# Streamed units shifted between the positions of a lap, and narrow convolution tiles cut to the pieces they need

## The chip, the cores and the metric

The kernel runs on one core of one Trainium2 chip. The metric is device time in microseconds (us) of one execution; lower is better. Engines: TensorE (PE; its weight loads are listed as PEld), VectorE (DVE), ScalarE (ACT), GpSimd (POOL), and SyncE (SP), which issues most loads.

## The reference

Two layers over x of shape 1 x 16 x 2048 x 2048 (f32):

```python
# layer 0: _gn is a group norm over pairs of channels; one 6 x 11 depthwise filter per channel
xm = where(tril(ones(H, W)), _gn(x), 0)
y  = conv(xm, weight, padding=((5, 0), (5, 5)), feature_group_count=C)
x  = x + where(tril(ones(H, W)), y, 0)
# layer 1: bias[c, i, j] = table[i - j + n - 1, c], table from a small network of the position
x  = x + (_gn(x) + bias)
```

So only the lower triangle of each channel is convolved and changed by layer 0, while both norms need sums over everything, and layer 1 touches every element.

## The kernel before

**Work.** A group is two channels (`CPG`), so there are 8 groups. A channel is cut into 4 bands of 512 rows; row = 4p + k, with p the partition and k = 0..3. The lower triangle of a band is walked in tiles of 128 columns that step by 118 (`STEP`): 5, 9, 13 and 18 tiles in bands 0 to 3, 45 per channel, 90 per group. Tile number n within the group, 0 to 89, is called its position (45 to 89 are the second channel). A tile is four pieces of 32 columns (`NPC`, `XC`). The last tile of a band is narrower: at positions 4, 44, 49 and 89 only two pieces hold columns of the band, at 13 and 58 three; the kernel before works on all four. A tile is "diagonal" (`is_diag`, 42 of 90) if it crosses the diagonal.

**A tile's way.** ACT normalizes it into `xn` (`norm`, L647, four tiles ahead); if diagonal, POOL multiplies `xn` by the mask (`mask_tile`, L1084); PE transposes four pieces into `psT` (L1170); ACT copies that as f16 into `XT` (`split_hi`, L659); DVE writes the f16 remainder (`split_lo`, L801); POOL moves two columns per piece through `halo` (L1099, L1110); PE does 36 matmuls into `psY`, nine per piece (L1184); DVE masks a diagonal tile in `psY` (L814) and adds it to x (`evict`, L816). `xn`, `psT`, `XT` and `psY` have three buffers each (`NB3`).

**Stages.** The program is a sequence of stages s, and each walks n = 0..89 on every engine. Stage s convolves group s - 1, collects the statistics of group s (bn_stats on DVE, L829) and finishes group s - 2 (norm 2 and bias). The time from the first eviction of a group to that of the next is called a lap here; laps 0 to 7 belong to groups 0 to 7.

**Streams.** What isn't held in SBUF passes through `ring`, 8 buffers of 512 KB. "a" units (58 per group, 0.5 MB loaded) are read for statistics by DVE: two bn_stats each. "u" units (36 per group, 0.5 MB loaded and 0.5 MB stored) are finished: 23 of them by ACT (scale, L708) and POOL (add bias, L1119), 13 by DVE alone (L1002). Kept blocks of bands 2 and 3 are finished in place by DVE (L991), stored by ACT's queue (L694), and then reloaded by SP for the next group (L572); `norm` of their first tile waits for the reload (tile 14, which ACT reaches at n = 10, and tile 18, at n = 14).

**The planner.** `plan` gives each u and a unit a position. `spread` fills, per position, the room that is left below a level after the other traffic; for u units the level is multiplied by `U_WEIGHT(n)`, and the a units are then spread with weight 1 over what the u units left. From these positions a loop over `wanted` fixes the ring buffer, the position of each load, use and store. A load of SP waits until the unit that held its buffer was stored or read, and SP's queue is in order: what stands behind it waits too. Stages 2 to 7 use this plan; in stages 8 and 9 the weight isn't used.

**PE's code.** Tiles go in triples, since buffers are taken modulo 3. Most triples run in hardware loops (`Fori`), the others are written out.

Of the kernel before, what the change touches and what calls it, by code (L numbers as in the profile page):

```python
# [25 lines left out]
def preact_conv_kernel(nc, x, wflip, w1, b1, w2, b2, w3, b3, out):  # L26
# [27 lines left out]
    def band_tiles(b):  # L54
# [73 lines left out]

    U_WEIGHT = lambda n: 1.8 if n < 10 else 1.5 if n > 82 else 1.0

# [177 lines left out]
    with ctx:  # L308
# [299 lines left out]
        def _(act):  # L608
# [45 lines left out]
            def split_hi(g, n):  # L654
                N = NT * g + n
                act.wait_ge(transposed, N + 1)
                wait(act, convolved, N - NB3 + 1)
                wait(act, halo_out, N - NB3 + 1)
                nc.scalar.copy(XT[:, n % NB3, 0, :, 2:P + 2], psT[n % NB3][:, :, :]).then_inc(hi_ready, 1)  # L659

# [119 lines left out]
        def _(dve):  # L780
# [282 lines left out]
        def _(pool):  # L1063
# [14 lines left out]
            def mask_tile(g, n):  # L1078
                c, b, t = TILES[n]
                pool.wait_ge(diag_normed, ND * g + DIAG_BEFORE[n] + 1)  # L1080
                v = xn[:, n % NB3, :, :, :]
                m = mask_at(b, t, 0, TIN)
                m = bass.AP(m.tensor, m.offset, [m.ap[0], [-XC, NPC], [1, K], [-1, XC]])
                nc.gpsimd.tensor_tensor(v, v, m, ALU.mult).then_inc(xn_ready, 1)  # L1084
# [16 lines left out]
            def halo_to(g, n):  # L1101

                c, b, t = TILES[n]
                N = NT * g + n
# [5 lines left out]
                nc.gpsimd.tensor_copy(halo[:, t, :, :, :], XT[:, n % NB3, :, :, P:P + 2]).then_inc(halo_out, 1)  # L1110

# [36 lines left out]
        def _(pe):  # L1148
# [15 lines left out]

            def transpose(N, m):

                wait(pe, lo_ready, N - NB3 + 1)
                pe.wait_ge(xn_ready, N + 1)
                for i in range(NPC):
# [19 lines left out]

            def triple(N, c, ahead=NB3, results_of=None):  # L1190

                for i in range(NB3):
                    if i < ahead:
                        transpose(N + i + 2, (i + 2) % NB3)
                    if i == 0 and results_of is not None:
                        sum_results(results_of)
                    convolve(N + i, i, c)

# [13 lines left out]
            def group(g, before, after):  # L1212

                first = NT * g
                pe.wait_ge(w_built, chan(g, 0) + 1)
                triple(first, 0, results_of=g - 1 if before else None)
                with pe.Fori(1, NTC // NB3) as j:
                    triple(first + NB3 * j, 0)
                pe.wait_ge(w_built, chan(g, 1) + 1)
                triple(first + NTC, 1)  # L1220
                with pe.Fori(NTC // NB3 + 1, SUM1[0] if after else 2 * NTC // NB3 - 1) as j:
                    triple(first + NB3 * j, 1)
                if after:
                    triple(first + NB3 * SUM1[0], 1)
                    sum_means(g + 1)
                    triple(first + NB3 * SUM1[1], 1)
                    sum_variances(g + 1)
                    with pe.Fori(SUM1[1] + 1, 2 * NTC // NB3 - 1) as j:
                        triple(first + NB3 * j, 1)

# [5 lines left out]
            for g in range(1, G - 1):  # L1236
                triple(NT * g - NB3, 1)
                group(g, True, True)
            triple(NT * (G - 1) - NB3, 1)
            group(G - 1, True, False)  # L1240
            triple(NT * G - NB3, 1, 1)
            sum_results(G - 1)
# [24 lines left out]
```

## Time and profile before

| what | value |
|---|---|
| median of 3 runs | 2638.41 us (2633.2 to 2640.93) |
| the profiled execution | 2638.45 us; its span 2636.7 us |
| DVE busy | 2304.3 us, 87% |
| PE busy | 1979.8 us, 75% |
| ACT / POOL busy | 1660.3 us, 63% / 1260.7 us, 48% |
| moved by DMA | 894.88 MB, mean 339 GB/s |

Busy time is the union of an engine's instructions; waiting, branching and issuing DMAs don't count. Group lines give count, busy time, mean duration, and the idle time before them with what ended it. In rows by stretch, DMA share is the mean busy share of the 16 DMA engines (it can come out slightly above 1), PEclk the granted TensorE clock.

### The profile page before, as it was taken

How to read it: one execution, taken by the hardware profiler on the slowest of the kernel's cores; microseconds unless marked ns; L12 is line 12 of the kernel's file. 1: busy time of each engine (PE TensorE's matmuls, PEld its weight loads, DVE VectorE, ACT ScalarE, POOL GpSimd, SP SyncE). 2: the span in 40 equal slices, each digit the busy share in tenths (PEclk: the TensorE clock that was granted, in tenths of full speed). 3: DMA queues.
4: the chain of work that ended last, by engine and by line, in shares of the span. 5: the costliest groups of instructions: out<-in, count | busy, mean ns of one | idle time of the engine just before them, and what ended most of it. 6: DMA issues, size and time to landing. Idle time of an engine off the chain costs nothing. (4 is left out here: it accounts for less than half of the span.)

```text
span 2636.7 us, 76763 instructions
## 1 busy us (share of the span) xinstructions
PE 1979.8 (75%) x28880; PEld 1876.5 (71%) x28880; DVE 2304.3 (87%) x4175; ACT 1660.3 (63%) x3051; POOL 1260.7 (48%) x1988
## 2 busy tenths in 40 slices
PE   4289988888687876878778877888868778899800
PEld 0289887878687776877778776787768778899800
DVE  7799988899888997899888998889988899778846
ACT  2167766766576675766667666666656757687722
POOL 1123235535545454454555445554554546475543
PEclk9999998999899999999898999999889998999955
DMA  9775649999899998999989998999989997797999
GB/s 337 273 243 170 233 136 384 393 371 351 329 408 377 380 337 332 402 359 385 354 334 396 359 366 329 378 392 362 348 329 395 384 373 297 284 355 274 334 370 360
DMA packets 313546, 894.88 MB, mean 339 GB/s; under 512 B 42272, under 2 KB 42272, under 8 KB 311296
## 3 DMA queue, kind: packets, MB, share of 16 engines
q1 hardware_dynamic: 198528, 576.64, 59.3%
q10 hardware_dynamic: 114832, 316.22, 31.0%
q8 instruction: 60, 0.98, 0.1%
q14 instruction: 126, 1.03, 0.1%
HBM read 576.36 MB, written 316.53 MB: 339 GB/s over the span
## 5 line engine op out<-in xcount | busy, mean ns | idle before, releaser
L1184 PEld LDWEIGHTS psY<-wsplit,XT 128*128 128x128 f16 x25920 | 1607.2, 102 | 355.9 <-DVE XT L801 128.6
L1184 PE MATMUL psY<-wsplit,XT 128*128 128x168 f16 (+5 forms) x25920 | 1635.9, 223 | 290.7 <-DVE XT L801 240.2
L659 ACT CAST XT<-psT 128x512 f16<-128x512 f32 x720 | 414.8, 576 | 561.0 <-PE psT L1170 325.5
L1110 POOL COPY halo<-XT 128x16 f16<-128x16 f16 x720 | 318.9, 443 | 657.5 <-DVE XT L801 647.3
L801 DVE TENSOR_TENSOR XT<-psT,XT 128x512 f16<-128x512 f32 x720 | 493.8, 686 | 140.3 <-ACT XT L659 139.4
L1084 POOL TENSOR_TENSOR xn<-xn,mask 128x512 f32<-128x512 f32 x336 | 423.7, 1261 | 387.5 <-ACT xn L647 325.8
L829 DVE BATCH_NORM_STATS2 entries<-ring 128x6 f32<-128x512 f32 x872 | 551.4, 679 | 61.3 <-DMA ring<-in_x 61.0
L1170 PE MATMUL psT<-ident,xn 128*128 128x128 f32 x2880 | 480.3, 292 | 98.2 <-POOL xn L1084 77.6
L1119 POOL TENSOR_TENSOR ring<-ring,bias 128x1024 f32<-128x1024 f32 x181 | 408.4, 2258 | 253.7 <-ACT ring L708 253.6
L647 ACT ACTIVATE xn<-kept_c_band,normp 128x512 f32<-128x512 f32 (+2 forms) x496 | 398.4, 803 | 48.3 <-DMA kept_c_band<-in_x 26.9
L1170 PEld LDWEIGHTS psT<-ident,xn 128*128 128x128 f32 x2880 | 317.8, 146 | 107.4 <-POOL xn L1084 72.5
L816 DVE SCALAR_TENSOR_TENSOR kept_c_band<-psY,wback,kept_c_band 128x472 f32<-128x472 f32 (+3 forms) x496 | 342.5, 691 | 14.2 <-PE psY L1184 7.3
L679 ACT ACTIVATE junk<-kept_c_band,cur 128x512 f32<-128x512 f32 (+2 forms) x464 | 311.6, 672 | 49.5 <-DVE kept_c_band L816 26.2
L991 DVE SCALAR_TENSOR_TENSOR kept_c_band<-kept_c_band,outp,bias 128x1024 f32<-128x1024 f32 x224 | 329.2, 1478 | 11.6 <-ACT bias L699 11.6
L708 ACT ACTIVATE ring<-ring,outp 128x1024 f32<-128x1024 f32 x181 | 206.0, 1140 | 124.1 <-DMA ring<-in_x 48.0
L814 DVE TENSOR_TENSOR psY<-psY,mask 128x472 f32<-128x472 f32 (+2 forms) x336 | 202.8, 604 | 11.7 <-PE psY L1184 11.4
L1002 DVE SCALAR_TENSOR_TENSOR ring<-ring,outp,bias 128x1024 f32<-128x1024 f32 x101 | 173.9, 1724 | 33.2 <-DMA ring<-in_x 24.3
L1099 POOL COPY XT<-halo 128x16 f16<-128x16 f16 x720 | 159.9, 222 | 51.4 <-PE psY L1184 47.4
L647 ACT ACTIVATE xn<-band,normp 128x512 f32<-128x512 f32 (+1 forms) x224 | 174.3, 779 | 13.9 <-DVE normp L911 13.9
L816 DVE SCALAR_TENSOR_TENSOR band<-psY,wback,band 128x472 f32<-128x472 f32 (+2 forms) x224 | 150.4, 671 | 6.3 <-PE psY L1184 0.7
L679 ACT ACTIVATE junk<-band,cur 128x512 f32<-128x512 f32 x192 | 131.9, 687 | 36.3 <-DVE band L816 27.1
L679 ACT ACTIVATION_READ_ACCUMULATOR junk<-kept_c_band,cur 128x1 f32 x464 | 87.1, 188 | 0.0
(81 smaller groups left out, 486.2 us busy)
## 6 DMA issues: line engine op xcount, KB each, us to landing
ring<-in_x SPq DMA_DIRECT2D x628, 512.0 KB, 8.6
out<-ring ACTq DMA_DIRECT2D x282, 512.0 KB, 6.1
kept_c_band<-in_x SPq DMA_DIRECT2D x224, 512.0 KB, 8.1
out<-kept_c_band ACTq DMA_DIRECT2D x224, 512.0 KB, 7.0
band<-in_x SPq DMA_DIRECT2D x48, 1024.0 KB, 11.3
out<-band ACTq DMA_DIRECT2D x45, 1024.0 KB, 8.7
ring<-out SPq DMA_DIRECT2D x90, 512.0 KB, 9.5
bias<-bias_scratch SPq DMA_DIRECT2D x16, 1793.5 KB, 8.5
```

The costliest lines, as they stand in the source:

```text
L647: last = nc.scalar.activation(to[:, :, 0:whole, :], slot(c, b)[:, :, x0:x0 + XC * whole].rearrange("p k (i c) -> p k i c", c=XC), ACT.Iden ...
L659: nc.scalar.copy(XT[:, n % NB3, 0, :, 2:P + 2], psT[n % NB3][:, :, :]).then_inc(hi_ready, 1)
L679: nc.scalar.activation(junk[:, 0:nr * (c1 - c0)].rearrange("p (r c) -> p r c", r=nr), slot(c, b)[:, r:r + nr, BW * q + c0:BW * q + c1], AC ...
L801: nc.vector.tensor_tensor(XT[:, n % NB3, 1, :, 2:P + 2], psT[n % NB3][:, :, :], XT[:, n % NB3, 0, :, 2:P + 2], ALU.subtract).then_inc(lo_r ...
L816: nc.vector.scalar_tensor_tensor(out=xs, in0=y, scalar=col(wback, c), in1=xs, op0=ALU.mult, op1=ALU.add, accum_out=sums[:, n:n + 1]).then_ ...
L829: last = nc.vector.bn_stats(entries[:, e, :], row(q, r))
L991: nc.vector.scalar_tensor_tensor(out=v, in0=v, scalar=col(outp, 0), in1=bias_at(blk, nr // 2 * h, nr // 2), op0=ALU.mult, op1=ALU.add).the ...
L1084: nc.gpsimd.tensor_tensor(v, v, m, ALU.mult).then_inc(xn_ready, 1)
L1110: nc.gpsimd.tensor_copy(halo[:, t, :, :, :], XT[:, n % NB3, :, :, P:P + 2]).then_inc(halo_out, 1)
L1119: nc.gpsimd.tensor_tensor(v, v, bias_at(STREAM[u]), ALU.add).then_inc(u_added, 1)
L1170: last = nc.tensor.transpose(psT[m][:, i, :], xn[:, m, i, :, :].rearrange("p k c -> p (k c)"), ident[:, :])
L1184: last = nc.tensor.matmul(psY[m][:, 0:rows, o + lo_c:o + hi_c], XT[:, m, xp, i, 2 - sh:2 - sh + P], wsplit[:, c, wp, K * sh:K * sh + rows, ...
```

## The change

Two things. The planner's weight of u units becomes 2.2 at positions 0 to 9 (was 1.8), 1.8 at 47 to 54 (was 1.0) and 1.2 from 83 on (was 1.5). And `split_hi`, `split_lo`, `halo_to`, the transposes and the convolution take `n_pieces[n]` pieces instead of four; `mask_tile` takes only the pieces from the diagonal's on, `evict` masks only the columns from the diagonal on. Since a loop of PE can't hold triples of different shape, `triples` loops only over runs of full ones (triples 5 to 13, 20 to 24, 27 and 28) and writes the others out.

```diff
+    n_pieces = [-(-min(TIN, BW * (b + 1) - STEP * t) // XC) for c, b, t in TILES]
+    left_of_diag = [max(0, BW * b - STEP * t) for c, b, t in TILES]
...
-    U_WEIGHT = lambda n: 1.8 if n < 10 else 1.5 if n > 82 else 1.0
+    U_WEIGHT = lambda n: 2.2 if n < 10 else 1.8 if 46 < n < 55 else 1.2 if n > 82 else 1.0
...
-                nc.vector.tensor_tensor(XT[:, n % NB3, 1, :, 2:P + 2], psT[n % NB3][:, :, :],
-                                        XT[:, n % NB3, 0, :, 2:P + 2], ALU.subtract).then_inc(lo_ready, 1)
+                np = n_pieces[n]
+                nc.vector.tensor_tensor(XT[:, n % NB3, 1, 0:np, 2:P + 2], psT[n % NB3][:, 0:np, :],
+                                        XT[:, n % NB3, 0, 0:np, 2:P + 2], ALU.subtract).then_inc(lo_ready, 1)
...
-                    nc.vector.tensor_tensor(y, y, mask_at(b, t, c0, c1), ALU.mult).then_inc(conv_masked, 1)
+                    d0 = max(c0, left_of_diag[n])
+                    y_diag = psY[n % NB3][:, :, d0:c1]
+                    nc.vector.tensor_tensor(y_diag, y_diag, mask_at(b, t, d0, c1), ALU.mult).then_inc(conv_masked, 1)
...
-                v = xn[:, n % NB3, :, :, :]
+                i0, i1 = left_of_diag[n] // XC, n_pieces[n]
+                v = xn[:, n % NB3, i0:i1, :, :]
...
-            def convolve(N, m, c):
+            def convolve(N, m, c, np=NPC):
...
-                products = [(i, sh, xp, wp) for i in range(NPC) for sh in range(3)
+                products = [(i, sh, xp, wp) for i in range(np) for sh in range(3)
...
+            def looped(j):
+                return all(n_pieces[(NB3 * j + i) % NT] == NPC for i in range(NB3 + 2))
```

By the new weights the units of stages 2 to 7 move. Per five positions, counts of uses before and after (a: statistics on DVE; D: u units finished by DVE; P: u units finished by ACT and POOL):

| positions | a | D | P |
|---|---|---|---|
| 0-4 | 5, 4 | 0, 0 | 2, 3 |
| 5-9 | 1, 1 | 1, 1 | 2, 3 |
| 10-14 | 1, 1 | 0, 0 | 1, 0 |
| 15-19 | 3, 3 | 0, 1 | 1, 0 |
| 20-24 | 5, 5 | 1, 0 | 0, 1 |
| 25-39 | 9, 9 | 2, 2 | 6, 6 |
| 40-44 | 6, 7 | 1, 1 | 1, 0 |
| 45-49 | 7, 5 | 0, 1 | 1, 2 |
| 50-54 | 2, 0 | 1, 0 | 0, 2 |
| 55-59 | 2, 1 | 0, 0 | 0, 0 |
| 60-64 | 3, 3 | 0, 0 | 0, 0 |
| 65-69 | 3, 4 | 0, 1 | 1, 0 |
| 70-74 | 2, 2 | 1, 0 | 2, 2 |
| 75-79 | 3, 4 | 1, 2 | 3, 2 |
| 80-84 | 3, 4 | 2, 2 | 3, 2 |
| 85-89 | 3, 5 | 3, 2 | 0, 0 |

The order on SP at the start of stage 4 (names: `ring` loads are a and u units, `kept_c0_band2` the reloads, `wstage` filter taps). Before:

```order
L566 DMA ring<-in_x 128x1024
L566 DMA ring<-in_x 128x2x512
L566 DMA ring<-in_x 128x1024
L572 DMA kept_c0_band2<-in_x 128x2x512 x2
L572 DMA kept_c0_band2<-in_x 128x1024
L592 DMA wstage<-taps_scratch 32x6x42 x4
L566 DMA ring<-in_x 128x1024
L572 DMA kept_c0_band2<-in_x 128x1024 x3
L566 DMA ring<-in_x 128x1024 x5
L572 DMA kept_c0_band3<-in_x 128x1024
```

And now:

```order
L570 DMA ring<-in_x 128x2x512 x2
L570 DMA ring<-in_x 128x1024 x4
L576 DMA kept_c0_band2<-in_x 128x2x512 x2
L576 DMA kept_c0_band2<-in_x 128x1024
L596 DMA wstage<-taps_scratch 32x6x42 x4
L576 DMA kept_c0_band2<-in_x 128x1024 x3
L570 DMA ring<-in_x 128x1024 x5
L570 DMA ring<-out_0 128x1024
L576 DMA kept_c0_band3<-in_x 128x1024
```

The ring load that stood between the taps and the second set of reloads is gone; the sixth and seventh u units (uses at n = 8 and 9, before at 13 and 18) now load ahead of the first reload. The last of them takes the buffer of this stage's first u unit, whose store is issued at n = 5.

On DVE, the same stage at tiles 48 to 50 (`psY0`, `psY1`, `psY2`), where L829 are the statistics and L991 the kept blocks. Before:

```order
L829 BN_STATS entries<-ring 128x6 x4
L814 TENSOR_TENSOR psY0<-psY0,mask 128x4x118
L816 SCALAR_TENSOR_TENSOR band0,sums<-psY0,wback,band0 128x4x118
L801 TENSOR_TENSOR XT<-psT0,XT 128x4x128
L991 SCALAR_TENSOR_TENSOR kept_c1_band2<-kept_c1_band2,outp,bias 128x1024
L829 BN_STATS entries<-ring 128x6 x4
L814 TENSOR_TENSOR psY1<-psY1,mask 128x4x35
L816 SCALAR_TENSOR_TENSOR band0,sums<-psY1,wback,band0 128x4x35
L801 TENSOR_TENSOR XT<-psT1,XT 128x4x128
L991 SCALAR_TENSOR_TENSOR kept_c1_band2<-kept_c1_band2,outp,bias 128x1024
L829 BN_STATS entries<-ring 128x6 x2
L816 SCALAR_TENSOR_TENSOR band1,sums<-psY2,wback,band1 128x4x123
```

And now:

```order
L837 BN_STATS entries<-ring 128x6 x2
L822 TENSOR_TENSOR psY0<-psY0,mask 128x4x118
L824 SCALAR_TENSOR_TENSOR band0,sums<-psY0,wback,band0 128x4x118
L807 TENSOR_TENSOR XT<-psT0,XT 128x4x128
L999 SCALAR_TENSOR_TENSOR kept_c1_band2<-kept_c1_band2,outp,bias 128x1024
L837 BN_STATS entries<-ring 128x6 x2
L822 TENSOR_TENSOR psY1<-psY1,mask 128x4x35
L824 SCALAR_TENSOR_TENSOR band0,sums<-psY1,wback,band0 128x4x35
L807 TENSOR_TENSOR XT<-psT1,XT 128x4x128
L999 SCALAR_TENSOR_TENSOR kept_c1_band2<-kept_c1_band2,outp,bias 128x1024
L824 SCALAR_TENSOR_TENSOR band1,sums<-psY2,wback,band1 128x4x123
```

Three pairs of statistics are gone from this short piece. On PE, tile 4 of the first group (`psY1`) is written out instead of being in the loop. Before, 36 matmuls in four pieces:

```order
L1184 MATMUL psY1<-wsplit,XT 128x4x37 x6
L1184 MATMUL psY1<-wsplit,XT 128x37 x3
L1184 MATMUL psY1<-wsplit,XT 128x4x42 x6
L1184 MATMUL psY1<-wsplit,XT 128x42 x3
L1184 MATMUL psY1<-wsplit,XT 128x4x42 x6
L1184 MATMUL psY1<-wsplit,XT 128x42 x3
L1184 MATMUL psY1<-wsplit,XT 128x4x32 x6
L1184 MATMUL psY1<-wsplit,XT 128x32 x3
```

And now, with the transposes around it, 18 in two:

```order
L1180 MATMUL psT0<-ident,xn 128x128 x4
L1194 MATMUL psY1<-wsplit,XT 128x4x37 x6
L1194 MATMUL psY1<-wsplit,XT 128x37 x3
L1194 MATMUL psY1<-wsplit,XT 128x4x42 x6
L1194 MATMUL psY1<-wsplit,XT 128x42 x3
L1180 MATMUL psT1<-ident,xn 128x128 x4
```

The third and fourth pieces are gone.

## Rows read from the trace of the kernel before

**Rows 1.** Laps 0, 3, 7: us, busy PE PEld DVE ACT POOL, PEclk, DMA share, GB/s.

```profile
125.20:384.20 259.00, 234.98 (x3682) 230.15 (x3679) 238.08 (x501) 179.31 (x359) 77.36 (x226) 0.97 0.58 195
1008.80:1321.60 312.80, 246.07 (x3606) 234.40 (x3606) 284.05 (x521) 205.43 (x380) 160.18 (x247) 0.92 0.96 365
2258.60:2497.80 239.20, 219.82 (x3468) 214.75 (x3468) 203.44 (x349) 192.05 (x356) 149.54 (x232) 0.98 0.87 320
```

**Rows 2.** Lap 3, positions 0-4, 10-14, 45-49, 65-69, 75-79, 80-84, 85-89.

```profile
1008.80:1027.20 18.40, 12.68 (x197) 11.67 (x198) 18.26 (x33) 10.37 (x16) 13.68 (x13) 1.00 0.64 213
...
1038.30:1060.30 22.00, 16.11 (x239) 15.72 (x238) 15.07 (x26) 13.57 (x27) 8.35 (x16) 0.84 1.03 415
...
1156.60:1177.90 21.30, 15.10 (x211) 13.60 (x209) 21.16 (x37) 13.27 (x21) 9.10 (x13) 0.92 0.89 342
...
1223.80:1244.20 20.40, 14.14 (x174) 13.16 (x175) 20.29 (x35) 11.10 (x22) 9.68 (x13) 0.83 0.96 378
...
1260.40:1275.80 15.40, 14.87 (x216) 14.60 (x216) 13.91 (x28) 10.51 (x19) 11.34 (x18) 0.90 0.78 292
1275.80:1294.60 18.80, 15.60 (x224) 14.56 (x222) 17.78 (x33) 11.10 (x22) 13.63 (x15) 0.91 0.98 343
1294.60:1321.60 27.00, 16.86 (x213) 16.06 (x210) 20.84 (x51) 15.89 (x36) 10.13 (x20) 0.81 0.98 387
```

**Rows 3.** Lap 3, positions 5-39 and 50-64; columns as in rows 1.

```profile
1027.20:1138.50 111.30, 92.92 (x1378) 90.08 (x1379) 93.56 (x173) 79.49 (x148) 59.72 (x94) 0.91 1.02 396
1177.90:1223.80 45.90, 38.29 (x604) 36.58 (x603) 44.20 (x81) 30.73 (x61) 19.83 (x38) 1.00 1.04 391
```

**Rows 4.** The timeline of ACT, its queue and DVE in lap 3.

```profile
1022.87 0.45 ACTq L716 DMA_DIRECT2D out<-ring  x1
...
1036.66 0.82 ACT L647 ACTIVATE xn<-kept_c_band,normp 128x512 f32<-128x512 f32 x1
...
1050.33 0.81 ACT L647 ACTIVATE xn<-kept_c_band,normp 128x512 f32<-128x512 f32 x1 [3.68 <-issue]
...
1052.74 1.29 DVE L829 BATCH_NORM_STATS2 entries<-ring 128x6 f32<-128x512 f32 x2 [6.08 <-DMA ring<-in_x]
```

**Rows 5.** SP's queue, lap 3: start, time to the last issue, what.

```profile
1017.06 9.06 SPq L572 DMA_DIRECT2D kept_c_band<-in_x  x3
...
1029.80 0.56 SPq L566 DMA_DIRECT2D ring<-in_x  x1
1035.92 8.12 SPq L572 DMA_DIRECT2D kept_c_band<-in_x  x3
```

**Rows 6.** Groups of lap 3 by shape: count, busy, mean ns.

```profile
L801 DVE TENSOR_TENSOR XT<-psT,XT 128x512 f16<-128x512 f32 x90 | 61.7, 686 | 13.9 <-ACT XT L659 13.9
...
L1002 DVE SCALAR_TENSOR_TENSOR ring<-ring,outp,bias 128x1024 f32<-128x1024 f32 x13 | 21.0, 1613 | 0.8 <-DMA ring<-out 0.8
L814 DVE TENSOR_TENSOR psY<-psY,mask 128x472 f32<-128x472 f32 x32 | 20.6, 643 | 0.2 <-PE psY L1184 0.2
...
L814 DVE TENSOR_TENSOR psY<-psY,mask 128x300 f32<-128x300 f32 x2 | 0.9, 466 | 0.0
```

**Rows 7.** PE's timeline, lap 3, two tiles in a loop.

```profile
1039.72 2.12 PE L1184 MATMUL psY<-wsplit,XT 128*128 128x148 f16 x36
...
1042.16 2.12 PE L1184 MATMUL psY<-wsplit,XT 128*128 128x148 f16 x36
```

**Rows 8.** Lap 0, positions 55 to 59; columns as in rows 1.

```profile
277.80:291.00 13.20, 13.20 (x220) 13.14 (x218) 12.72 (x27) 11.41 (x24) 1.85 (x10) 1.00 0.82 271
```

**Rows 9.** DMA in lap 3: totals; issues, KB each, median us to landing.

```profile
DMA packets 39495, 114.30 MB, mean 365 GB/s; under 512 B 4912, under 2 KB 4912, under 8 KB 39216
...
out<-ring ACTq DMA_DIRECT2D x36, 512.0 KB, 6.4
...
kept_c_band<-in_x SPq DMA_DIRECT2D x28, 512.0 KB, 7.7
```

**Rows 10.** DVE's timeline at the end of lap 3.

```profile
1316.42 0.69 DVE L801 TENSOR_TENSOR XT<-psT,XT 128x512 f16<-128x512 f32 x1 [5.16 <-ACT XT L659]
```

More of the change, by code:

```diff
@@ L658, in split_hi @@
                 wait(act, halo_out, N - NB3 + 1)
-                nc.scalar.copy(XT[:, n % NB3, 0, :, 2:P + 2], psT[n % NB3][:, :, :]).then_inc(hi_ready, 1)
+                np = n_pieces[n]
+                nc.scalar.copy(XT[:, n % NB3, 0, 0:np, 2:P + 2], psT[n % NB3][:, 0:np, :]).then_inc(hi_ready, 1)
             def copy_edge(g, n, w):
@@ L1080, in mask_tile @@
                 pool.wait_ge(diag_normed, ND * g + DIAG_BEFORE[n] + 1)
-                v = xn[:, n % NB3, :, :, :]
-                m = mask_at(b, t, 0, TIN)
-                m = bass.AP(m.tensor, m.offset, [m.ap[0], [-XC, NPC], [1, K], [-1, XC]])
+                i0, i1 = left_of_diag[n] // XC, n_pieces[n]
+                v = xn[:, n % NB3, i0:i1, :, :]
+                m = mask_at(b, t, XC * i0, TIN)
+                m = bass.AP(m.tensor, m.offset, [m.ap[0], [-XC, i1 - i0], [1, K], [-1, XC]])
                 nc.gpsimd.tensor_tensor(v, v, m, ALU.mult).then_inc(xn_ready, 1)
@@ L1103, in halo_to @@
                 c, b, t = TILES[n]
+                np = n_pieces[n]
                 N = NT * g + n
@@ L1109, in halo_to @@
                         wait_alone(pool, edge_copied, 16 * K * (NEDGE * g + edges_before(n)))
-                nc.gpsimd.tensor_copy(halo[:, t, :, :, :], XT[:, n % NB3, :, :, P:P + 2]).then_inc(halo_out, 1)
+                nc.gpsimd.tensor_copy(halo[:, t, :, 0:np, :], XT[:, n % NB3, :, 0:np, P:P + 2]).then_inc(halo_out, 1)
             def add_bias(g, u):
@@ L1163, in _, with transpose @@
             pe.wait_ge(const_ready, 7)
-            def transpose(N, m):
+            def transpose(N, m, np=NPC):
                 wait(pe, lo_ready, N - NB3 + 1)
                 pe.wait_ge(xn_ready, N + 1)
-                for i in range(NPC):
+                for i in range(np):
                     last = nc.tensor.transpose(psT[m][:, i, :], xn[:, m, i, :, :].rearrange("p k c -> p (k c)"), ident[:, :])
                 last.then_inc(transposed, 1)
-            def convolve(N, m, c):
+            def convolve(N, m, c, np=NPC):
                 pe.wait_ge(lo_ready, N + 1)
@@ L1188, in convolve, with triple, triples @@
                 last.then_inc(convolved, 1)
-            def triple(N, c, ahead=NB3, results_of=None):
+            def triple(N, c, ahead=NB3, results_of=None, first=None):
+                pieces = [NPC if first is None else n_pieces[(first + i) % NT] for i in range(NB3 + 2)]
                 for i in range(NB3):
                     if i < ahead:
-                        transpose(N + i + 2, (i + 2) % NB3)
+                        transpose(N + i + 2, (i + 2) % NB3, pieces[i + 2])
                     if i == 0 and results_of is not None:
                         sum_results(results_of)
-                    convolve(N + i, i, c)
+                    convolve(N + i, i, c, pieces[i])
+            def looped(j):
+                return all(n_pieces[(NB3 * j + i) % NT] == NPC for i in range(NB3 + 2))
+            def triples(first, c, lo, hi):
+                while lo < hi:
+                    end = lo
+                    while end < hi and looped(end):
+                        end += 1
+                    if end - lo > 1:
+                        with pe.Fori(lo, end) as j:
+                            triple(first + NB3 * j, c)
+                    else:
+                        end = lo + 1
+                        triple(first + NB3 * lo, c, first=NB3 * lo)
+                    lo = end
             def sum_means(g):
@@ L1215, in group @@
                 pe.wait_ge(w_built, chan(g, 0) + 1)
-                triple(first, 0, results_of=g - 1 if before else None)
-                with pe.Fori(1, NTC // NB3) as j:
-                    triple(first + NB3 * j, 0)
+                triple(first, 0, results_of=g - 1 if before else None, first=0)
+                triples(first, 0, 1, NTC // NB3)
                 pe.wait_ge(w_built, chan(g, 1) + 1)
-                triple(first + NTC, 1)
-                with pe.Fori(NTC // NB3 + 1, SUM1[0] if after else 2 * NTC // NB3 - 1) as j:
-                    triple(first + NB3 * j, 1)
+                triples(first, 1, NTC // NB3, SUM1[0] if after else 2 * NTC // NB3 - 1)
                 if after:
-                    triple(first + NB3 * SUM1[0], 1)
+                    triples(first, 1, SUM1[0], SUM1[0] + 1)
                     sum_means(g + 1)
-                    triple(first + NB3 * SUM1[1], 1)
+                    triples(first, 1, SUM1[1], SUM1[1] + 1)
                     sum_variances(g + 1)
-                    with pe.Fori(SUM1[1] + 1, 2 * NTC // NB3 - 1) as j:
-                        triple(first + NB3 * j, 1)
+                    triples(first, 1, SUM1[1] + 1, 2 * NTC // NB3 - 1)
             sum_means(0)
@@ L1236, in _ @@
             for g in range(1, G - 1):
-                triple(NT * g - NB3, 1)
+                triple(NT * g - NB3, 1, first=NT - NB3)
                 group(g, True, True)
-            triple(NT * (G - 1) - NB3, 1)
+            triple(NT * (G - 1) - NB3, 1, first=NT - NB3)
             group(G - 1, True, False)
-            triple(NT * G - NB3, 1, 1)
+            triple(NT * G - NB3, 1, 1, first=NT - NB3)
             sum_results(G - 1)
```

1 line of the change is left out of this document (added).

## The prediction

> **What bounds the kernel now.** I read the busy time by lap first, then one lap by five positions, then what ends the idle time of DVE there, and last the queue that feeds it. Laps 1 to 6 have the same program, and lap 3 stands for them: DVE is busy 284.05 of 312.8 us, and the DMA engines' mean share is 0.96. PE has 246.07 and isn't the bound. Lap 0 (259 us) has no u units, lap 7 (239.2 us) no statistics; there PE is busy 234.98 and 219.82 us, 91 and 92% [rows 1]. So two resources are nearly full in a usual lap, and DVE's 28.7 us of idle time say how much a better order could win at most from DVE's side.
>
> By positions they take turns [rows 2, 3]. At 0-4 DVE is full (18.26 of 18.4) and DMA is not (0.64). At 5-39 the DMA share is 1.02 for 111.3 us and DVE idles 17.7 us; the largest piece is the wait for a ring load of 6.08 us at position 13 [rows 4]. At 50-64 both are full: DVE 44.2 of 45.9, DMA 1.04. At 45-49 and from 65 on DVE leads (21.16 of 21.3 us, and 20.29 of 20.4 at 65-69), with 1.5 and 1.0 us idle at 75-79 and 80-84 and 6.2 us at 85-89, of which 5.16 us are one wait at the lap's end, for PE and ACT [rows 10]. The reader is to see that DVE work removed at 0-4, 40-49 or 65 on is time won, and that the same work removed where the DMA share is 1 may not be.
>
> **The narrower work.** A mask instruction takes 643 ns for 472 columns and 466 for 300 [rows 6]: 177 ns for 172 elements, 1.03 ns each. Per channel the masks lose 35 columns at position 9, 75 at 22 and 115 at 39, times four rows: 900 elements, 0.93 us. The remainder's row (686 ns for 512 elements) has one shape only, so a piece of 128 elements costs between nothing and a quarter, 0.17 us; I take the mask's slope, nearest in form (both read PSUM), 0.13 us. Ten pieces a group: 1.3 us. DVE loses 3.2 us per group, 25.4 in 8 groups. Where do they land?
> - Laps 1 to 6, where DVE is full and DMA less: the halved tiles 4, 44, 49, 89 (0.26 each) and the masks at 67 and 84 (0.31, 0.48): 1.8 us a lap, 11 in six.
> - The same laps at 9, 13, 22, 39, 54, 58, 1.4 us a lap, lie where DMA is full. I count 0.4 (position 22, DVE full too), 2.4 in six; bounds 0 and 8.
> - Laps 0 and 7. PE is busy 13.20 of 13.20 us at 55-59 of lap 0 [rows 8]. A full tile costs PE 2.44 us (1039.72 to 1042.16), 0.61 a piece [rows 7]. Tiles 13 and 58 lose one piece each where PE is full, 1.2 us in each lap; with tile 44 of lap 7 (1.2) and the DVE items that lie on full DVE, some 2.3 and 3.2 us: 5.5.
>
> The sum is 19 us of gain, with bounds 10 and 28. POOL loses 22 pieces of mask a group and ACT 10 of its copy: both are under 66% busy in lap 3 [rows 1], so I cost them at nothing. If POOL were on the path, its gain would come on top.
>
> PE's loops are replaced at nine triples a group by written-out code. In the loop of the row PE goes from tile to tile in 2.44 us with no gap [rows 7], and written-out triples exist before too. I take nothing.
>
> **The moved units.** No byte is added. DVE's share: a pair of statistics is 1.29 us [rows 4], a u unit on DVE 1.61 [rows 6]. From the table of uses: 0-4 one pair less, -1.3; 5-39 the same number, 0; 40-49 one pair less and one unit more, +0.3; 50-64 three pairs and one unit less, -5.5; 65-89 five pairs more, +6.5. What of it is time:
> - 65-89: 2.5 us of idle time at 75-84 can take some, +4.0 (bounds 0.5, if the end's wait takes 3.5 more, and 6.5).
> - 50-64: DMA is full. If all is DVE's, -5.5; if DMA alone sets the pace, 0. The share of 1.04 speaks for DMA, DVE's 44.2 of 45.9 for DVE: I take half, -2.7.
> - 0-4 and 40-49: -1.0.
>
> That is +0.3 a lap, between -6 and +5.5; in six laps +2, between -36 and +33 if every lap were at the same end. I hold one half of these ends to be within reach, -18 to +17.
>
> **The queue past which a load moves.** At the start of a stage SP now issues two u loads ahead of the first reload, and the second needs the buffer of the first u unit, stored at n = 5. In the trace the first reload goes out at 1017.06 [rows 5]; that store is issued at 1022.87 [rows 4], and with the median of 6.4 us to landing [rows 9] it is there at about 1029.3. So the first reload goes out about 12 us later, and behind it wait the taps, four more reloads and the a loads. The reload's user, `norm` of tile 14, ran at 1036.66 [rows 4]: 7.4 us are left for a transfer whose median is 7.7 [rows 9], just enough. The second three reloads wait for stores of kept blocks anyway (from 1035.92 over 8.12 us [rows 5]), and `norm` of tile 18 started at 1050.33 after 3.68 us idle [rows 4]. In exchange no statistics stand at n = 13 any more: DVE can do the work of n = 14 during that wait. I take the two to cancel; the end of the cost is priced as a rival. POOL now adds three u units in a row at n = 7 to 9 where it added one; what that holds up at tiles 10 to 12 is hidden by the 6.08 us that DVE waits at 13, as long as that wait remains.
>
> **The sum.** Against the profiled execution of 2638.45 us (span 2636.7, 1.8 outside it; the median is 2638.41, so nothing is to be converted): 2638.4 - 19 + 2 = 2621, rounded 2620. Its own range goes from 2598 to 2640.
>
> **Rivals.**
> - *DMA sets the pace of every usual lap* (0.20). For it: the share of 0.96 over a lap and full stretches of 111 and 46 us. Against: 415 GB/s is reached at 10-14 [rows 2], and at that rate the 114.30 MB of a lap [rows 9] need 275 us, not 313; and 0-4 has a share of 0.64. Then no removed instruction of DVE helps in laps 1 to 6, only the 5.5 us of laps 0 and 7 do: 2633, no difference that can be told. The Trainium skill, DMA: Bandwidth & Descriptors, section Bandwidth, says that between HBM and SBUF the limit is the HBM side, about 358 GB/s. By that rule a lap needs 114.30 MB / 358, 319 us, more than it takes, and the change could bring nothing; the trace disagrees with the figure (365 over the lap, 415 in a stretch), so I keep only the weaker form.
> - *The reloads come late* (0.20), slower. The mechanism is the load that waits on SP for the store of the stage's first u unit. Three transfers more (a load, a store, the moved reload, 1.5 MB) then stand ahead of the kept stores: 3.8 us at 396 GB/s [rows 3]. It decides once the first set lands after 1036.66, or the second after 1050.33 [rows 4]. All of it on the path: 3.8 x 6 = 23; with the DVE work at 65-89 unrelieved, as the full DMA at 50-64 then has it (+2.7 x 6 = 16): 2621 + 39 = 2660. Half of that is 2641; I give 2652.
> - *The smoothing works* (0.18), more gain. The wait of 6.08 us at position 13 [rows 4] is there because loads queue behind the reloads; with no statistics at n = 13 and fewer units at 10-24 it shrinks, and at 50-64 most of the 5.5 us are kept. With 3 us a lap from the one and 2.7 more from the other: 34 us, 2587.
> - *The written-out code stalls PE* (0.03). The Trainium skill, Runtime: NRT & Kernel Launch, section Instruction fetch mechanics, says the opposite: code is fetched ahead in sequence, and it is a taken branch that may stall. No row here shows a stall of either kind.
>
> **How the numbers follow.** The sum above gets 0.39. Faster by over 0.3% (below 2630.5; three runs of the kernel before spread over 0.3%, and less can't be told from no change) is the most of it (0.35) and all of the smoothing (0.18): 0.54 with a little of the DMA rival. Slower by over 0.3% (above 2646.3) is 0.2 from the late reloads, and little else: 0.23. Within it remains 0.23. The range that leaves 2 in 10 out takes half of the smoothing's and most of the late reloads' values: 2590 to 2656.
>
> **What the profile after would show.** DVE busy about 25 us less (2304 to 2279). PE about 50 us less: 80 pieces of 0.61. Masks of 128x332, 128x172 and 128x12 beside 128x472. If the sum holds, laps 0 and 7 are 2 to 3 us shorter each and laps 1 to 6 about 2 us each, with 0-4 and 50-64 shorter and 65-89 longer. For the DMA rival laps 1 to 6 keep 312 to 313 us, and DVE's idle time grows by what it lost. For the late reloads SP issues its first reload more than 10 us after the one of before, and ACT idles before `norm` of tile 14 or 18. For the smoothing, DVE's wait for ring loads falls by 20 us or more in all.
>
> The prediction would be wrong above all if DVE's work at 65-89 finds no idle time, or if the two ends of the SP queue don't cancel.

## The result, and the profile after

| | before | after |
|---|---|---|
| median of 4 runs | 2638.33 us | 2657.93 us |
| range of the runs | 2633.20 to 2640.93 | 2657.05 to 2665.19 |
| ratio of after to before, 95% interval | | 1.0083 [1.0059, 1.0106] |
| span of the profiled execution | 2636.7 us | 2657.0 us |

The change makes the kernel 0.8% slower, where 0.7% faster was forecast; 2657.93 us lies 2 us above the range. The first lines of the page after:

```profile
span 2657.0 us, 74659 instructions
PE 1931.1 (73%) x28080; PEld 1823.3 (69%) x28080; DVE 2276.0 (86%) x4175; ACT 1649.2 (62%) x3051; POOL 1212.1 (46%) x1988
```

Before, DVE was busy 2304.3 us and PE 1979.8: 28.3 us less on DVE (25.4 were forecast) and 48.7 us less on PE (about 50). These totals match partly by luck, since both also move where no work is removed (e7_written_out, below, runs the matmuls of before and has PE busy 1958.7 us, at a mean granted clock of 0.923 where the traced run of before has 0.912; the instruction that finishes a u unit on DVE, L1002 before and L1010 after, takes between 1.27 and 3.37 us, and its 101 fell from 173.9 to 149.6 us in sum). The two groups that the forecast was about are the firm evidence: the masks (L814, now L822) went from 202.8 to 188.1 us and the remainders (L801, now L807) from 493.8 to 483.7, together 24.8 us. So the work did leave, and the time did not follow. Laps 0, 3 and 7 after, with the columns of [rows 1]:

```profile
126.00:389.10 263.10, 231.14 (x3580) 225.65 (x3577) 240.78 (x509) 178.50 (x359) 72.34 (x226) 0.94 0.60 201
1021.90:1339.20 317.30, 241.29 (x3506) 230.09 (x3506) 280.42 (x523) 203.79 (x380) 154.19 (x247) 0.92 0.96 361
2282.20:2519.70 237.50, 213.10 (x3370) 208.06 (x3370) 198.75 (x350) 191.07 (x357) 144.80 (x232) 0.99 0.89 323
```

Lap 3 is 4.5 us longer although DVE has 3.6 us less to do: DVE's idle time grew from 28.7 to 36.9 us. Lap 0 is 4.1 us longer, lap 7 1.7 us shorter. Lap 0 has no u units, and yet the weights changed it: its DVE row has 509 instructions where it had 501, which are four pairs of statistics more. The a units are spread over the room that the u units leave, and their plan is the same in every stage that has them, so more statistics of the next group fall into lap 0 and as many fewer into lap 6 (501 before, and now 494):

```profile
1975.00:2282.20 307.20, 240.90 (x3506) 230.08 (x3506) 265.80 (x494) 203.28 (x380) 153.38 (x247) 0.92 0.90 339
```

So "the units of stages 2 to 7 move" was true of the u units only. Four pairs are 5.2 us at 1.29 us a pair; lap 6 is only 1.7 us shorter. The other laps, from first eviction to first eviction: lap 1 311.8 to 316.2 us, lap 2 312.8 to 316.6, lap 4 313.7 to 319.6, lap 5 314.4 to 316.2, lap 6 308.9 to 307.2. The mean of laps 1 to 5 by positions:

| positions | before | after |
|---|---|---|
| 0-4 | 18.4 | 19.4 |
| 5-9 | 11.9 | 15.6 |
| 10-19 | 33.9 | 34.0 |
| 20-44 | 83.1 | 81.9 |
| 45-54 | 34.5 | 31.8 |
| 55-59 | 18.0 | 22.3 |
| 60-64 | 14.9 | 15.1 |
| 65-89 | 98.3 | 97.1 |

The loss is in two places, 5-9 and 55-59, each at or right behind positions with more u units. Windows of lap 3 after, positions 0-4, 5-9 and 10-19; columns as in [rows 1]:

```profile
1021.90:1041.30 19.40, 12.90 (x178) 12.29 (x179) 19.23 (x33) 10.21 (x16) 13.56 (x13) 0.91 0.50 175
1041.30:1056.90 15.60, 10.66 (x120) 10.16 (x120) 9.97 (x20) 8.90 (x15) 9.27 (x11) 0.78 1.03 378
1056.90:1090.90 34.00, 30.83 (x470) 30.18 (x470) 30.16 (x53) 24.82 (x49) 17.39 (x31) 0.95 1.04 411
```

At 0-4 DVE is still full, but the DMA share has fallen from 0.64 to 0.50 [rows 2]: for some 19 us the DMA engines are half empty, and then they are full. At 5-9 DVE is idle for 5.6 of 15.6 us. The timeline of SP's queue in lap 3 after shows why the DMA engines had little to do (start, time, what was issued):

```profile
1008.42 33.25 SPq L570 DMA_DIRECT2D ring<-in_x  x6
1041.76 4.42 SPq L576 DMA_DIRECT2D kept_c_band<-in_x  x3
1046.28 5.01 SPq L596 DMA_DIRECT2D wstage<-taps_scratch  x4
1051.38 7.97 SPq L576 DMA_DIRECT2D kept_c_band<-in_x  x3
```

The first reload goes out at 1041.76, 19.9 us into the lap; before it was 8.3 us (1017.06 in [rows 5], lap start 1008.8). That is 11.6 us later, and 12 were forecast. The load ahead of it waits for the store of the stage's first u unit. That store and what follows stand in ACT's timeline:

```profile
1036.98 0.45 ACTq L721 DMA_DIRECT2D out<-ring  x1
...
1041.04 4.98 ACTq L721 DMA_DIRECT2D out<-ring  x3
1046.13 0.59 ACT L664 CAST XT<-psT 128x512 f16<-128x512 f32 x1 [5.67 <-PE psY L1194]
...
1057.15 0.81 ACT L651 ACTIVATE xn<-kept_c_band,normp 128x512 f32<-128x512 f32 x1 [2.03 <-POOL xn L1093]
```

ACT issues three stores over 4.98 us, of units that others finish, and runs nothing of its own until 1046.13. It doesn't wait for these units: POOL had added its two by 1035.48 and DVE had finished the third at 1040.18. The issues themselves are long, 1.87, 1.35 and 1.68 us by their own rows, against 0.45 for the one at 1036.98, while SP issues its three reloads at some 1.5 us each. POOL then starts its mask after 6.07 us of idle time:

```profile
1047.51 2.11 POOL L1093 TENSOR_TENSOR xn<-xn,mask 128x512 f32<-128x512 f32 x1 [6.07 <-ACT xn L651]
```

The last row of ACT is `norm` of tile 14, the user of the first reload. It starts 35.3 us into the lap instead of 27.9, but what it waits for is POOL, not the reload. The wait at position 13 is gone, as forecast: over positions 10-19 DVE now waits 0.8 us for ring loads. So the lateness of the reload is plain, and whether it costs anything can't be read here; that needed runs.

A second thing had changed, on PE and in the queue that carries code. Page and chain of waits, before and then after:

```profile
q8 instruction: 60, 0.98, 0.1%
PEld psT L1170 <- issue: 6.0, 5, 2.0
```

```profile
q8 instruction: 123, 2.02, 0.3%
PEld psT L1180 <- issue: 62.6, 44, 4.1
```

The columns of the second row are us, times, and the longest. Ahead of its transposes PE now waits 44 times, 62.6 us in all, for nothing that the profile names, and 2.02 instead of 0.98 MB of instructions come in by q8. The prediction had put this at nothing.

### The profile page after: what moved, and what is told of

It is laid out like the page before. It is cut to its first block and busy times, and to the rows that moved or that the text cites. A ratio compares the mean times of both kernels' runs of the same rounds, so it can differ in the third digit from the quotient of the medians.

```text
span 2657.0 us, 74659 instructions
## 1 busy us (share of the span) xinstructions
PE 1931.1 (73%) x28080; PEld 1823.3 (69%) x28080; DVE 2276.0 (86%) x4175; ACT 1649.2 (62%) x3051; POOL 1212.1 (46%) x1988
## 3 DMA queue, kind: packets, MB, share of 16 engines
q8 instruction: 123, 2.02, 0.3%
## 5 line engine op out<-in xcount | busy, mean ns | idle before, releaser
L1194 PEld LDWEIGHTS psY<-wsplit,XT 128*128 128x128 f16 x25200 | 1562.4, 102 | 359.0 <-DVE XT L807 198.7
L1194 PE MATMUL psY<-wsplit,XT 128*128 128x128 f16 (+5 forms) x25200 | 1591.1, 223 | 290.3 <-DVE XT L807 244.3
L664 ACT CAST XT<-psT 128x512 f16<-128x512 f32 x720 | 405.8, 564 | 550.2 <-PE psT L1180 304.9
L807 DVE TENSOR_TENSOR XT<-psT,XT 128x512 f16<-128x512 f32 x720 | 483.7, 672 | 142.0 <-ACT XT L664 141.0
L1093 POOL TENSOR_TENSOR xn<-xn,mask 128x512 f32<-128x512 f32 (+2 forms) x336 | 385.0, 1146 | 431.5 <-ACT xn L651 392.9
L1180 PE MATMUL psT<-ident,xn 128*128 128x128 f32 x2800 | 469.9, 291 | 148.0 <-POOL xn L1093 94.8
L1180 PEld LDWEIGHTS psT<-ident,xn 128*128 128x128 f32 x2800 | 308.0, 146 | 158.3 <-issue 62.6
L684 ACT ACTIVATE junk<-kept_c_band,cur 128x512 f32<-128x512 f32 (+2 forms) x464 | 311.8, 672 | 97.1 <-DVE kept_c_band L824 74.0
L822 DVE TENSOR_TENSOR psY<-psY,mask 128x472 f32<-128x472 f32 (+3 forms) x336 | 188.1, 560 | 28.1 <-PE psY L1194 28.1
L1010 DVE SCALAR_TENSOR_TENSOR ring<-ring,outp,bias 128x1024 f32<-128x1024 f32 x101 | 149.6, 1483 | 53.1 <-DMA ring<-in_x 48.0
## 6 DMA issues: line engine op xcount, KB each, us to landing
band<-in_x SPq DMA_DIRECT2D x48, 1024.0 KB, 10.5
out<-band ACTq DMA_DIRECT2D x45, 1024.0 KB, 11.2
```

Of the source, the lines that this page charges most:

```text
L664: nc.scalar.copy(XT[:, n % NB3, 0, 0:np, 2:P + 2], psT[n % NB3][:, 0:np, :]).then_inc(hi_ready, 1)
L684: nc.scalar.activation(junk[:, 0:nr * (c1 - c0)].rearrange("p (r c) -> p r c", r=nr), slot(c, b)[:, r:r + nr, BW * q + c0:BW * q + c1], AC ...
L807: nc.vector.tensor_tensor(XT[:, n % NB3, 1, 0:np, 2:P + 2], psT[n % NB3][:, 0:np, :], XT[:, n % NB3, 0, 0:np, 2:P + 2], ALU.subtract).then ...
L1194: last = nc.tensor.matmul(psY[m][:, 0:rows, o + lo_c:o + hi_c], XT[:, m, xp, i, 2 - sh:2 - sh + P], wsplit[:, c, wp, K * sh:K * sh + rows, ...
```

## The experiments

All ratios are times to the kernel before on the same chip, with the 95% interval. What a single trace shows is one execution, and executions of one kernel differ by up to 20 us here (e3_early_old: 2631.31 to 2651.68), so positions and waits are read for where a thing happens, and the price is taken from the ratio. Two runs split the change. For the first, the kernel after gets the old weights back:

```diff
-    U_WEIGHT = lambda n: 2.2 if n < 10 else 1.8 if 46 < n < 55 else 1.2 if n > 82 else 1.0
+    U_WEIGHT = lambda n: 1.8 if n < 10 else 1.5 if n > 82 else 1.0
```

> The changed kernel with the old weights: only the narrower work and the written-out triples of TensorE are left of the change. If the moved units cost the time (theory 1), this gains what was forecast for the narrower work, 10 to 20 us: 2618 to 2628 us. If the pieces or the written-out code cost it (theory 2), it is as slow as the whole change, 2650 to 2660 us.

Measured: 2632.87 us, 0.9998 [0.9987, 1.0010]. The narrow tiles and masks with PE's new code are worth nothing in sum, short of the gain that my first theory gave them. The second is the kernel before with the new weights, the same lines the other way.

> The kernel before with the new weights alone. Theory 1: slower than the whole change, since nothing of the narrower work helps it: 2665 to 2680 us. Theory 2: as the kernel before or faster, 2630 to 2640 us.

Measured: 2658.86 us, 1.0086 [1.0071, 1.0102]. The moved units alone are the whole loss, though the time is 6 us under the range of my first theory. Laps 1 to 5 of its trace are 4.6 us longer in the mean: 4.9 at 0-9, 1.3 at 55-59, nothing at 65-89 (98.3 and 98.3), and the rest takes 1.6 back. So the 5-9 of the table above is the moved units' own, and of the 4.3 us at 55-59 only 1.3 show here; e1_pieces_only, without them, has 1.3 there too. The granted clock is no rival: its mean over the runs was 0.919 in this kernel and 0.920 in the kernel before.

**Which weight.** Four kernels are the one after with one or two of the three weights as they were:

| kernel | weight 0-9 | 47-54 | 83-89 | us | ratio |
|---|---|---|---|---|---|
| e3_early_old | 1.8 | 1.8 | 1.2 | 2642.25 | 1.0022 [1.0005, 1.0039] |
| e4_middle_old | 2.2 | 1.0 | 1.2 | 2662.59 | 1.0105 [1.0088, 1.0122] |
| e14_late_only | 1.8 | 1.0 | 1.2 | 2638.86 | 1.0020 [1.0006, 1.0033] |
| e15_middle_only | 1.8 | 1.8 | 1.5 | 2650.15 | 1.0058 [1.0037, 1.0080] |

> The changed kernel with the weight 1.8 instead of 2.2 at positions 0 to 9; the u units of the first ten positions stand as before, 47 to 54 and 83 on stay changed. If the load that waits at the head of the stage for the first unit's store is the whole cost (theory 1a), this takes 2620 to 2632 us and positions 0 to 19 take as long as before (60.3 us of lap 3). If it is the second channel's part (theory 1b), 2648 us or more.

> The changed kernel with the weight 1.0 instead of 1.8 at positions 47 to 54; the early units stay moved. Theory 1a: as slow as the whole change, 2650 to 2660 us. Theory 1b: 2620 to 2635 us. If both parts cost about half, this and the run with the old early weight both lie near 2640 us.

> The changed kernel with only the last part of the weights changed (1.2 instead of 1.5 from 83 on; 1.8 at 0 to 9, 1.0 at 47 to 54, as before). Without any new weight it was 0.9998 of the kernel before, with the middle and last part 1.0022. If the last part costs it: 1.001 to 1.003. If it is nothing: 0.999 to 1.001.

> The changed kernel with only the middle part of the weights changed (1.8 at 47 to 54). If this part costs the 0.24%: 1.001 to 1.004; if it gains, as it seemed to beside the early part (1.0105 without it, 1.0083 with it): 0.996 to 0.999.

The base of all four is e1_pieces_only at 0.9998. e3_early_old lies between its two theories, and its positions 0-19 are 3.5 us a lap shorter than before (60.7 for 64.2; the 60.3 in its expectation was a slip, lap 3 had 64.4); e15_middle_only missed both of its ranges, from above. The weight at 0-9 is the largest part: taking it back in the change saves 0.6% (1.0083 to 1.0022), and with the one at 83-89 alone it costs 0.85% (1.0105 against 1.0020). The others don't add up: the late weight costs 0.2% alone, the middle one 0.6% alone, both together 0.2%, and beside the early one the middle one seems to give 0.2% back (1.0105 to 1.0083, less than their intervals can tell apart). A weight moves units over its channel and statistics over the whole lap, not only where it is written. Lap 0 shows it: 256.1 to 257.1 us in the traces of e1, e4, e14 and e16, which have the narrow tiles and the old middle weight, 260.6 in e15, and 262.4 to 264.0 in the five kernels with the new middle and late weights.

**The order on SP.** In SP's stage the reloads of a position go ahead of its u loads:

```diff
+                    if do_b:
+                        for blk in KEPT:
+                            for h in range(2):
+                                if reload_pos(blk, h) == n and gb > 0:
+                                    load_kept(gb, blk, h)
...
-                        for blk in KEPT:
-                            for h in range(2):
-                                if reload_pos(blk, h) == n and gb > 0:
-                                    load_kept(gb, blk, h)
```

> The whole change, with SP's queue mended at one point: at each position the reloads of kept blocks go out ahead of the u loads, so that the first two reloads (position 6) no longer stand behind the u load that waits for the first unit's store. The reloads of positions 9 and 10 and the taps still do. If the place of those two reloads is what costs (theory 1a), positions 0 to 19 fall from 69.0 us by 2 to 4 us and the total is 2640 to 2650 us. If it is the work itself of the moved units (POOL's three in a row, ACT's scaling, DMA stores), nothing moves: 2655 to 2662 us.

Measured on the kernel after: 2641.65 us, 1.0039 [1.0026, 1.0052]. Half of the loss is gone, but not where it was expected: positions 0-19 stay at 68.6 us a lap (69.0), 20-44 go from 81.9 to 79.7 and 45-64 from 69.3 to 67.4. The DMA share at 0-4 of lap 3 is back at 0.63:

```profile
1013.10:1032.60 19.50, 12.23 (x182) 11.16 (x182) 19.36 (x30) 10.12 (x16) 13.57 (x13) 1.00 0.63 195
```

The counter-test adds the wait to the kernel before and moves no unit:

```diff
+                    if do_c and do_b and n == 6 and not stays(gc, 0):
+                        u0 = ("u", gc, 0)
+                        wait_alone(sp, u_stored[buffer_of[u0]], 16 * store_count[u0])
```

> The kernel before with one wait more: at position 6 SP waits for the store of the stage's first u unit before it goes on to the reloads. No unit is moved. If the late reloads are the cost of the early weight (theory 1a), this alone costs most of its 17 us: 2648 to 2656 us. If the moved units' work costs it, 2634 to 2640 us.

Measured: 2644.51 us, 1.0044 [1.0028, 1.0060]. SP's timeline in lap 3 of this kernel:

```profile
1002.17 19.00 SPq L569 DMA_DIRECT2D ring<-in_x  x5
1032.39 2.92 SPq L575 DMA_DIRECT2D kept_c_band<-in_x  x3
1035.42 4.99 SPq L595 DMA_DIRECT2D wstage<-taps_scratch  x4
```

From 1021.17 to 1032.39 SP issues nothing, and 12 us are lost over the kernel though no other instruction has changed. That is between the two ranges that were expected. This lateness has a price of its own, and nothing cancels it. At 0-4 the same work takes the same 18.4 us as before, with the DMA share at 0.49 instead of 0.64:

```profile
1014.50:1032.90 18.40, 12.63 (x197) 11.63 (x198) 18.23 (x32) 10.40 (x16) 13.64 (x13) 1.00 0.49 178
```

The loss stands behind it: 10-19 grow by 1.4 us a lap and 20-44 by 0.7. Positions 5-9 don't grow (11.7 us for 11.9), and in e5_reload_first, where the share is restored, they stay at 14.9. So the loss at 5-9 is not SP's order but something else in the moved units.

But the order isn't all of the early part. With the middle weight old and the reloads first:

> The changed kernel with the old weight at 47 to 54 and the reloads ahead of the u loads of a position: the slowest of the weights so far (1.0105) with SP's order mended. If the queue's order is most of what the early part costs, 1.003 to 1.006, as it was with the middle part changed too (1.0083 to 1.0039). If that gain came from the second channel, it stays above 1.008.

Measured: 2658.99 us, 1.0087 [1.0061, 1.0113] against 1.0105 without the reordering. That is the second of the two expected outcomes: 0.2% comes back, which the two intervals can't tell from nothing. So most of the early weight's 0.85% has another cause there, and what the reordering gives depends on the middle weight.

**The pieces without PE.** Old weights, all narrow work on ACT, DVE and POOL, and PE's block as it was before, loops and full tiles:

```diff
-            def transpose(N, m, np=NPC):
+            def transpose(N, m):
...
-                triple(first, 0, results_of=g - 1 if before else None, first=0)
-                triples(first, 0, 1, NTC // NB3)
+                triple(first, 0, results_of=g - 1 if before else None)
+                with pe.Fori(1, NTC // NB3) as j:
+                    triple(first + NB3 * j, 0)
```

> Old weights; narrow tiles on ACT, DVE and POOL, but TensorE with its four pieces and its loops as before. If written-out code eats the gain of the narrower work (theory 2), this is faster than the kernel before by 10 to 20 us, 2615 to 2625 us. If the narrower work gains nothing because laps 1 to 6 are paced by something else (theory 3), 2628 to 2638 us.

Measured: 2624.18 us, 0.9960 [0.9947, 0.9974]. The narrow work does gain, 0.40% or 10.5 us (8.2 from median to median). Its line of statistics in the groups, before and then here:

```profile
L829 DVE BATCH_NORM_STATS2 entries<-ring 128x6 f32<-128x512 f32 x872 | 551.4, 679 | 61.3 <-DMA ring<-in_x 61.0
```

```profile
L837 DVE BATCH_NORM_STATS2 entries<-ring 128x6 f32<-128x512 f32 x872 | 552.0, 680 | 77.6 <-DMA ring<-in_x 77.2
```

DVE's busy time fell by 33 us in this execution (2304.3 to 2271.1), of which masks and remainders are 25.2, and its span by 13.3; DVE waits 16 us longer for ring loads. It is likely that removed DVE work goes there in a lap whose DMA share is 0.96, but not shown: e7_written_out and e9_all_written, below, remove none and wait 12 and 23 us longer.

**PE's code alone.** The kernel before, with nine triples a group written out as in the change, all tiles full:

```diff
+            def looped(j):
+
+                return all(n_pieces[(NB3 * j + i) % NT] == NPC for i in range(NB3 + 2))
...
-                with pe.Fori(1, NTC // NB3) as j:
-                    triple(first + NB3 * j, 0)
+                triples(first, 0, 1, NTC // NB3)
```

> The kernel before, with TensorE's triples written out as in the change and every tile at its full four pieces. Theory 2: slower than before by 8 to 18 us, 2643 to 2653 us. Theory 3: no difference, 2630 to 2640 us.

Measured: 2646.80 us, 1.0062 [1.0042, 1.0082]. The same instructions run on the same data, and 14 us are lost in the median of six. Its rows of the page and of the waits, and then those of the kernel below in which no loop is left:

```profile
q8 instruction: 129, 2.11, 0.3%
PEld psT L1171 <- issue: 27.4, 43, 2.0
```

```profile
q8 instruction: 231, 3.78, 0.6%
PEld psT L1170 <- issue: 115.4, 91, 4.8
```

PE's nameless waits ahead of a transpose go from 6.0 us before to 27.4 and 115.4, with 0.98, 2.11 and 3.78 MB of instructions. But these waits are not the price. The traced execution of e7_written_out took 2640.36 us, the fastest of its six and only 1.9 us more than the traced one of before, and its laps 1 to 5 are as long as before (313.1 us); e1_pieces_only has 35.1 us of them in an execution of 2625.00 us. So no trace here shows where the 14 us go. Two kernels vary the number of triples written out. With only the first channel's (five a group):

```diff
-                return all(n_pieces[(NB3 * j + i) % NT] == NPC for i in range(NB3 + 2))
+                return j > NTC // NB3 or all(n_pieces[(NB3 * j + i) % NT] == NPC for i in range(NB3 + 2))
```

> The kernel before with only the first channel's triples 1 to 4 and 14 written out (5 a group instead of 9), full tiles. Writing out 9 cost 0.62%, writing out 25 cost 0.72%. If each place where code has to be loaded at the start of a band costs about the same, 0.3 to 0.4%: 2642 to 2645 us. If the cost is there as soon as the code exceeds some amount, 0.5 to 0.7%: 2647 to 2652 us.

Measured: 2639.52 us, 1.0022 [1.0007, 1.0037], below both ranges. With no loop at all (25 triples a group more than before):

```diff
-                with pe.Fori(1, NTC // NB3) as j:
+                for j in range(1, NTC // NB3):
```

> The kernel before with every triple of TensorE written out: 25 looped triples a group become code, where the change wrote out 9. Writing out the 9 cost 0.62%. If the cost goes with the amount of code that has to be loaded (theory 2a), this costs 25/9 of it, 1.7%: 2670 to 2685 us. If it is a cost of short loops beside written-out code (theory 2b), it vanishes with the last loop: 2632 to 2642 us.

Measured: 2652.55 us, 1.0072 [1.0048, 1.0096]. So 5, 9 and 25 triples cost 0.2, 0.6 and 0.7%: more code costs more from 5 to 9, but not in proportion, and 9 and 25 can't be told apart; the last lies between the two theories. PE's waits did grow fourfold from 9 to 25; the time hardly did.

**The pieces put together again.** New weights, reloads first, PE as before; then the same with the old weights:

> All three findings together on the changed kernel: its weights, the reloads ahead of the u loads of a position, narrow tiles everywhere but on TensorE, whose loops are as before. If they add up (0.39% with the reloads mended, less 0.38% for TensorE's code): 2628 to 2636 us. If the moved units' work still costs with the code gone, 2638 us or more.

> Old weights, narrow tiles but on TensorE (2624 us), and the reloads ahead of the u loads of a position. With the old weights the load ahead of the first reload waits for a statistics unit and not for a store, so the order should matter little: 2620 to 2626 us. A gain of over 0.2% would say that SP's order costs in the kernel before too.

Measured: 2634.54 us, 0.9999 [0.9984, 1.0014], and 2628.02 us, 0.9987 [0.9974, 1.0000]. With the reloads first in both, the moved units cost 0.1%, against 0.9% in their own. With the old weights the reordering gains nothing, and may cost 0.3% (0.9960 without it; expected were 2620 to 2626 us): it mends only what the new ones broke. Against e6_pieces_not_pe, the best order without moved units, they still cost 0.4%.

Last, e6_pieces_not_pe with PE narrow only in triples that were written out before (transposes of tiles 4, 49 and 89, convolution of 89):

```diff
-                triple(first, 0, results_of=g - 1 if before else None)
+                triple(first, 0, results_of=g - 1 if before else None, first=0)
...
-                triple(first + NTC, 1)
+                triple(first + NTC, 1, first=NTC)
```

> Old weights, narrow tiles but on TensorE, and on TensorE only in the triples that were written out before: three transposes and one convolution a group (tiles 4, 49, 89). No line of code is added. If TensorE's narrower work is worth its share where it costs no code: 2620 to 2624 us, at or below the 2624 us without it.

Measured: 2620.97 us, 0.9949 [0.9931, 0.9967], q8 at 0.95 MB. This one beats both kernels: the narrow work at half a per cent, with no code added and no unit moved.

## Why the prediction was wrong

**The busy times** were right where they can be read by group: masks and remainders 24.8 us less for 25.4. PE's 48.7 for 50 is a match within some 20 us that PE's total moves by itself.

**The narrower work, "19 us of gain".** Right within what the runs can tell. With PE's code written out in both, it is the step from 1.0062 (e7_written_out) to 0.9998 (e1_pieces_only): 0.64%, 17 us. Without PE's part it is 10.5 us (e6_pieces_not_pe); laps 1 to 5 are 1.4 us shorter there, from 313.1 to 311.7 in the mean, where 2.2 were forecast, and lap 0, whose share was PE's, is not. The rival in which DMA sets the pace of every usual lap left at most 5.5 us, 0.2%, and all of it in laps 0 and 7; a gain of 0.40% [0.26, 0.53] without PE's part speaks against it. The 16 us of longer waits for ring loads suggest that DMA takes its part.

**PE's code, "I take nothing".** This step failed; 0.62% was its price, 14 us from median to median, as much as the narrow work gives: that is why the two sum to nothing in e1_pieces_only. The prediction argued that PE goes through its loop without a gap and that written-out triples exist already. Neither says what more of them cost. The rival that had them stall PE got 0.03. It named the Trainium skill, Runtime: NRT & Kernel Launch, section Instruction fetch mechanics, where sequential code is fetched ahead and a taken branch may stall; in this kernel the loops were the cheaper form, and the measurement decides. How the code costs time stays open. That instructions come late, behind data on DMA engines with a share near 1, is a guess: q8's bytes and PE's nameless waits do rise together, but the time of an execution doesn't follow these waits, and no run took away the data's traffic.

**The moved units, "+2 us".** This is the term that broke the sum: the weights alone cost 0.86%, 23 us. The sum had +0.3 us a lap; with the weights alone (e2_weights_only) laps 1 to 5 are 4.6 longer. By the stretches of the sum:

| positions | forecast | weights alone | whole change |
|---|---|---|---|
| 0-4 and 40-49 | -1.0 | -0.4 | -1.4 |
| 5-39 | 0 | +4.1 | +3.6 |
| 50-64 | -2.7 | +0.9 | +3.1 |
| 65-89 | +4.0 | 0.0 | -1.3 |

The two ends that I feared were the wrong ones. The cost stands at 5-39, most of it at 5-9 (3.4 and 3.7), to which the sum gave no time because DVE's work there stays the same; and the gain at 50-64 didn't come. Lap 0, forecast 2 to 3 us shorter, is 4.1 longer, with four pairs of statistics that the sum didn't have there. A sum by the DVE work of each stretch doesn't see what the stretch waits for.

**The SP queue, "I take the two to cancel".** This step failed too. The reload went out 11.6 us later, as worked out, and the wait at position 13 did disappear, but the delay has a price (0.44% in e8_wait_added, and 0.44% back in e5_reload_first) and the freed wait paid nothing for it: 10-19 take 34.0 us for 33.9. That is about half of the loss. The rival "the reloads come late" had the right queue and 2652 us. Its test was wrong: `norm` of tile 14 did start late, but behind POOL, and the loss shows later in the lap. What goes with the cost in all three kernels is the DMA share at 0-4: 0.50 in the change, 0.49 with the wait alone, 0.63 with the order mended, for 0.64 before. That it is made up in stretches where the share is 1 fits the places of the loss.

**What stays open.** With the middle weight old, most of the early weight's cost isn't the order on SP (e16_middle_old_reload_first). The trace offers ACT's queue: three store issues of 1.35 to 1.87 us in a row, beside those of SP, delay the `split_hi` and `norm` on which 5-9 depend (DVE's idle time there is for `split_hi`, 4.5 us of 5.6), with three units in a row on POOL at n = 7 to 9. This was not tried by a run. Also open: why the weights' parts don't add, where the written-out code's time goes, and why 25 written-out triples cost hardly more than 9.

## What to carry to other kernels

- Where an in-order queue issues the loads, look at what a moved load stands in front of, and price the time in which the queue issues nothing: DMA engines that idle early in a lap are missed where they are full, far from the place of the wait.
- Unrolling a hardware loop on one engine isn't free because its instructions stay the same; look at the bytes of the instruction queue before and after, and time the unrolled form alone, several executions of it, with nothing else changed. Waits with no releaser in one trace didn't give the price here.
- Where one plan serves all stages, check also the stages that don't have the units you move: here the statistics moved in lap 0.
- Split a change whose parts have nothing to do with each other. Here narrow work at 0.5% gain was hidden under code and units that cost more.

## What the runs showed of the hardware

Written-out code has a price that PE's busy time doesn't show: with nine more triples a group the page's q8 carried 2.11 MB instead of 0.98, and the kernel was 0.62% slower (14 us from median to median); with 3.78 MB 0.72% (19 us). PE's waits without a releaser ahead of transposes were 6.0, 27.4 and 115.4 us in the traced executions, whose times were 2638.45, 2640.36 and 2650.26 us: most of the added waiting cost nothing.

A queue that issues nothing for 11.2 us early in each usual lap cost 0.44% (e8_wait_added), with the DMA share at 0-4 down from 0.64 to 0.49 and DVE as busy there as before.

The issue of a 512 KB store on ACT's queue took 0.45 us at 1036.98 in lap 3 after, and 1.35 to 1.87 us when three stood in a row while SP issued reloads of 1.5 us each; ACT ran nothing of its own meanwhile.
